# The first normalisation of x, taken from a second copy of x with channels on partitions

## The reference

```
x = x + tanh(g_xattn) * xattn(layernorm(x), ctx, ctx)        # 16 heads of 16, softmax, Wq Wk Wv Wo
x = x + tanh(g_ffn)   * ffn(layernorm(x))
layernorm(x) = (x - mean) / sqrt(var + 1e-5)                 # over the 256 channels, no weights
ffn(h):  h = bit_linear(h, w1)                               # 256 -> 1024
         h = depthwise_conv1d(h, 3 taps over positions) + b
         h = silu(h)
         return bit_linear(h, w2)                            # 1024 -> 256
bit_linear(x, w): x rounded to 8 bits per token, w to -1, 0, 1, then x @ w.T
```

## Time and profile before

| | |
|---|---|
| time of the runs | median 223.53 us, 222.73 to 223.77, 3 runs |
| profiled execution | 222.88 us, of which the span in the profile is 221.1 us |
| busy, share of the span | TensorE 92%, VectorE 82%, ScalarE 72%, GpSimd 62% |
| granted TensorE clock | 0.992 of full speed |
| largest chain shares | TensorE 64%, GpSimd 12%, VectorE 11% |
| DMA | 12.99 MB in 22159 packets, 59 GB/s over the span |

### The profile page before, as it was taken

One profiled execution on the slowest core, in us unless ns is written; L12 is line 12 of the kernel. 1 busy time (PEld: TensorE's weight loads), 2 busy tenths in 40 slices (PEclk: granted clock), 3 DMA queues, 4 the chain that ended last, 5 costly groups with the idle time before them and its releaser, 6 DMA issues.

```text
span 221.1 us, 6179 instructions
## 1 busy us (share of the span) xinstructions
PE 204.3 (92%) x2300; PEld 167.8 (76%) x2312; DVE 182.0 (82%) x375; ACT 160.1 (72%) x318; POOL 136.8 (62%) x241
## 2 busy tenths in 40 slices
PE   7999899999899999999999999999889849998894
PEld 7978778778688878788887878888558737786783
DVE  4154557698969899999999999999999989998982
ACT  2358677787678888897979888785689945875541
POOL 2502322553727575766758576675657998999971
PEclk9999999999999999999999999999999988999999
DMA  5992010101101010101100000000001222555543
GB/s 150 347 335 81 21 49 3 49 10 42 31 19 50 3 49 3 47 8 44 27 3 1 4 0 3 0 4 0 3 0 43 55 47 73 122 100 164 123 132 104
DMA packets 22159, 12.99 MB, mean 59 GB/s; under 512 B 13682, under 2 KB 21874, under 8 KB 22130
## 3 DMA queue, kind: packets, MB, share of 16 engines
q1 hardware_dynamic: 22130, 12.60, 20.0%
HBM read 7.36 MB, written 2.10 MB: 43 GB/s over the span
## 4 chain that ended last, share of the span: by engine, by line
PE 64%; POOL 12%; DVE 11%; issue 10%; ACT 1%; DMA 1%; POOLq 0%; ACTq 0%; DVEq 0%
PE ps_score L558 9%; PE ps_proj L524 8%; PE ps_proj L603 6%; PE ps_max L568 6%; PE ps_av L581 6%; PE ps_proj L516 5%; POOL y L415 5%; PE ps_proj L507 5%; PE ps_h L662 4%; POOL w2f L403 3%; PE ps_av L489 3%; DVE smax L1146 3%; PE ps_av L591 3%; PE ps_proj L495 2%; DVE zmax L1320 2%
## 5 line engine op out<-in xcount | busy, mean ns | idle before, releaser
L1146 DVE TENSOR_REDUCE smax<-ps_max 128x8 f32<-128x1024 f32 x31 | 37.9, 1224 | 14.1 <-PE ps_max L568 10.7
L910 ACT ACTIVATE prob<-ps_score 128x1024 f32<-128x1024 f32 x32 | 32.8, 1023 | 17.8 <-PE ps_score L558 16.9
L558 PE MATMUL ps_score<-Qs,KT 32*128 32x128 f32 x512 | 37.1, 283 | 2.0 <-DVE smax L1146 0.8
L558 PEld LDWEIGHTS ps_score<-Qs,KT 32*128 32x128 f32 x512 | 31.3, 186 | 9.3 <-issue 5.0
L568 PE MATMUL ps_max<-KT,QT 32*128 32x256 f32 x248 | 35.1, 400 | 0.0
L382 POOL TENSOR_SCALAR xn<-xn,qa 128x256 f32<-128x256 f32 x16 | 8.6, 535 | 27.0 <-DVE qa L1186 26.9
L568 PEld LDWEIGHTS ps_max<-KT,QT 32*128 32x128 f32 x248 | 21.2, 184 | 0.1
L403 POOL TENSOR_SCALAR w2f<-y,zmax 128x1024 f16<-128x1024 f32 x16 | 17.9, 1118 | 2.3 <-DVE zmax L1325 1.0
L1320 DVE TENSOR_REDUCE zmax<-y 128x1 f32<-128x1024 f32 x16 | 19.3, 1206 | 0.0
L524 PE MATMUL ps_proj<-xnT,wq 128*128 128x128 f32 x128 | 18.3, 286 | 0.9 <-ACT xnT L884 0.6
L1202 DVE SCALAR_TENSOR_TENSOR y<-hid,conv,y 128x508 f32<-128x508 f32 x24 | 19.1, 801 | 0.0
(11 more groups left out here) (147 smaller groups left out, 526.6 us busy)
## 6 DMA issues: line engine op xcount, KB each, us to landing
cin<-ctxT SPq DMA_DIRECT2D x16, 128.0 KB, 2.1
xres<-x SPq DMA_DIRECT2D x16, 128.0 KB, 2.5
out<-xres SPq DMA_DIRECT2D x16, 128.0 KB, 1.8
w1f<-w1T SPq DMA_DIRECT2D x1, 1024.0 KB, 7.0
w2f<-w2T SPq DMA_DIRECT2D x1, 1024.0 KB, 9.0
wk<-wkT SPq DMA_DIRECT2D x1, 256.0 KB, 2.8
wv<-wvT SPq DMA_DIRECT2D x1, 256.0 KB, 4.5
wq<-wqT SPq DMA_DIRECT2D x1, 256.0 KB, 4.7
```

The source lines that it names most:

```text
L558: mm = pe.matmul(ps_score[:, i * 512 + j * P:i * 512 + (j + 1) * P], KT[b % 3][rows, j * P:(j + 1) * P], Qs[rows, j * P:(j + 1) * P], star ...
L910: act.activation(prob[pair][:, :], ps_score[:, :], ACT.Exp, scale=DH ** -0.5).then_inc(exp_done, 1)
L1146: dve.tensor_reduce(dst, first_max(n, pair)[:, :].rearrange("p (g t e k) -> p g t e k", g=PG, t=KD, e=2), AX.X, ALU.max).then_inc(max_done, 1)
```

## The change

1. A second array `xT` comes in with each sequence of x laid out with channels on partitions. For sequences 4 to 15 (`BY_DMA = 4`) it is loaded into one of three buffers `xT` (`XB = 3`), and GpSimd normalises it there: one product with the factors, one sum with the shifts, both 128x256. project_q reads that buffer. TensorE's transposes and ScalarE's copy stay for sequences 0 to 3 only.
2. With channels on partitions, factor and shift differ along a row and are the same on all partitions. GpSimd makes them for several sequences at once (`norm_rows`, batches of 1, 1, 2, 4, 6 and 2 sequences, four small instructions each). For sequences 4 to 15 SP writes them to DRAM in three DMAs (`write_rows`), element by element, and loads two rows of 128 back for each sequence with all 128 partitions getting the same (`load_rows`), into one of two buffers `norm_bc`.
3. All statistics are VectorE's: those of sequences 2 to 13 in steps 0 to 2 and ahead of them, 14 and 15 in steps 7 and 8. ScalarE's sum_x and square_x are gone.
4. The last tap of tiles 1, 3, ... 17 is shared as those from 20 on: ScalarE makes the product behind its raw copy in the next step, and GpSimd adds it at the end of that step, behind norm1.
5. The loads of x come earlier, those of w2, of the small constants and of contexts 3 and on later; contexts 5 and on stand behind waits for `norm_ready` and `rows_out`.

```diff
+            def load_xT(n):
+                wait(sp, q_ready, n - XB + 1)
+                sp.dma_start(xT[n % XB][:, :], xTd[n * P:(n + 1) * P, :]).then_inc(xT_in[n % XB], 16)
+
+            def write_rows(first, last, ready):
+                sp.wait_ge(norm_ready, ready)
+                sp.dma_start(norm_dram[2 * first:2 * last, :].rearrange("r p -> p r"),
+                             norm_row[:, 2 * first:2 * last],
+                             allow_slow_non_contiguous=True).then_inc(rows_out, 16)
+
+            def load_rows(n, batches):
+                sp.wait_ge(rows_out, 16 * batches)
+                wait(sp, xn_done, n - 1 if n >= BY_DMA + 2 else 0)
+                sp.dma_start(norm_bc[n % 2][:, :],
+                             norm_dram[2 * n:2 * n + 2, :].rearrange("r p -> (r p)").partition_broadcast(P)
+                             ).then_inc(bc_in[n % 2], 16)
...
             load_x(2)
+            load_x(3)
             load_c(2)
+            load_x(4)
+            load_x(5)
+            load_c(3)
             load_w(w1f, w1T, KD, w1_in)
-            load_x(3)
-            load_c(3)
+            load_x(6)
+            load_x(7)
+            load_w(wo, woT, KD, wo_in)
+            for i in range(8, NB):
+                load_x(i)
+            sp.dma_start(conv[:, :], cwb).then_inc(small_in, 16)
             load_w(w2f, w2T, NC_, w2_in)
-            load_w(wo, woT, KD, wo_in)
-            sp.dma_start(conv[:, :], cwb).then_inc(small_in, 16)
-            for i in range(4, NB):
-                load_x(i)
-                load_c(i)
+            for n in range(BY_DMA, BY_DMA + XB):
+                load_xT(n)
+            load_c(4)
+            write_rows(4, 8, 4)
+            load_rows(4, 1)
+            load_rows(5, 1)
+            load_c(5)
+            load_c(6)
+            write_rows(8, 14, 5)
+            load_rows(6, 2)
+            load_c(7)
+            load_xT(7)
+            load_rows(7, 2)
+            for n in range(8, NB):
+                load_c(n)
+                load_xT(n)
+                if n == 14:
+                    write_rows(14, NB, 6)
+                load_rows(n, 2 if n < 14 else 3)
...
+            def norm_rows(first, last, batch):
+                k = slice(first, last)
...
+                gp.wait_ge(mv1_done, last)
+                gp.tensor_scalar(var1[:, k], var, EPS_LN, None, ALU.add).then_inc(norm_step, 1)
+                gp.wait_ge(norm_step, 3 * batch + 1)
+                gp.tensor_tensor(rstd, var1[:, k], minus_half[:, k], ALU.pow).then_inc(norm_step, 1)
+                gp.wait_ge(norm_step, 3 * batch + 2)
+                gp.tensor_tensor(mean_rstd1[:, k], mean, rstd, ALU.mult).then_inc(norm_step, 1)
+                gp.wait_ge(norm_step, 3 * batch + 3)
+                gp.tensor_scalar(shift, mean_rstd1[:, k], -1.0, 1.0, ALU.mult, ALU.mult).then_inc(norm_ready, 1)
...
             def norm1(i):
...
+                gp.wait_ge(xT_in[i % XB], 16 * ((i - BY_DMA) // XB + 1))
+                gp.wait_ge(bc_in[i % 2], 16 * ((i - BY_DMA) // 2 + 1))
+                gp.tensor_tensor(x3, x3, rstd, ALU.mult).then_inc(scaled_x, 1)
+                gp.wait_ge(scaled_x, i - BY_DMA + 1)
+                gp.tensor_tensor(x3, x3, shift, ALU.add).then_inc(xn_done, 1)
...
                 if seq(s + 2):
                     norm1(s + 2)
-                if seq(s + 3):
-                    gp.wait_ge(sh1_done, s + 3)
-                    x_mean(s + 3)
+                if s == 0:
+                    norm_rows(4, 8, 3)
+                if s == 2:
+                    norm_rows(8, 14, 4)
+                if s == 9:
+                    norm_rows(14, NB, 5)
+                for T in TILES.get(s - 1, ()):
+                    if tap_on_gp(T):
+                        add_tap(T)
...
             def project_q(n):
-                pe.wait_ge(xT_done, n + 1)
+                if n < BY_DMA:
+                    pe.wait_ge(xT_done, n + 1)
+                else:
+                    pe.wait_ge(xn_done, n + 1)
+                    pe.wait_ge(x1_done, n - 2)
...
                 for T in tiles[0:1]:
                     raw_copy(T)
+                for T in last[1:2]:
+                    if tap_on_gp(T):
+                        outer_product(T)
                 exponent(b, 0)
...
             def outer_taps(T):
                 first_tap(T)
-                last_tap(T)
+                if not tap_on_gp(T):
+                    last_tap(T)
...
+            stats_of(2, 3)
             row_max(0, 1)
-            step(0)
-            step(1)
+            step(0, lambda k: stats_of(4, 5) if k == 1 else None)
+            step(1, lambda k: stats_of(6, 7) if k == 0 else stats_of(8, 9))
...
+            def in_step2(k):
+                if k == 0:
+                    stats_of(10, 11)
+                else:
+                    weight_scale(0)
+                    stats_of(12, 13)
...
+            step(SB + 3, lambda k: stats_of(14) if k == 1 else None)
+            step(SB + 4, lambda k: stats_of(15) if k == 1 else None)
```

More of the change, by code:

```diff
@@ L49 @@
 ON_GP = 20
+BY_DMA = 4
+XB = 3
 BY_PE = 12
@@ L253, in turned, with tap_on_gp, tap_buffer @@
             return 16 * (v // ZT + 1)
+        def tap_on_gp(T):
+            return T >= ON_GP or T % 2 == 1 and T < ON_GP - 2
         def gp_taps(T):
-            return T - ON_GP + 1
+            return sum(tap_on_gp(t) for t in range(T + 1))
         def finished(eng, T):
-            eng.wait_ge(conv_done, min(T + 1, ON_GP))
+            eng.wait_ge(conv_done, T + 1 - gp_taps(T))
             wait(eng, conv_gp, gp_taps(T))
+        def tap_buffer(T):
+            return by_sequence(tap[gp_taps(T) % 2][:, :])[:, :, 0:P - 1]
         @block.sync
@@ new lines, in norm1 @@
+            def norm1(i):
+                if i < BY_DMA:
+                    gp.wait_ge(norm_ready, min(i, 2) + 1)
+                    wait(gp, xT_ready, i - 1)
+                    gp.tensor_scalar(xn[i % 2][:, :], xres[:, i * D:(i + 1) * D], norm_row[:, 2 * i:2 * i + 1],
+                                     norm_row[:, 2 * i + 1:2 * i + 2], ALU.mult, ALU.add).then_inc(xn_done, 1)
+                    return
+                x3 = xT[i % XB][:, :].rearrange("p (k n) -> p k n", n=P)
+                rstd, shift = (norm_bc[i % 2][:, e * P:(e + 1) * P].unsqueeze(1).broadcast_to([P, KD, P]) for e in range(2))
+                gp.wait_ge(xT_in[i % XB], 16 * ((i - BY_DMA) // XB + 1))
[3 more added lines that the diff above has]
+                gp.tensor_tensor(x3, x3, shift, ALU.add).then_inc(xn_done, 1)
@@ L520, in project_q @@
             def project_q(n):
-                pe.wait_ge(xT_done, n + 1)
+                if n < BY_DMA:
[3 more added lines that the diff above has]
+                    pe.wait_ge(x1_done, n - 2)
+                source = xnT if n < BY_DMA else xT[n % XB]
                 for t in range(KD):
@@ L524, in project_q @@
                         mm = pe.matmul(ps_q[:, t * P:(t + 1) * P], wq[:, k * D + t * P:k * D + (t + 1) * P],
-                                       xnT[:, k * P:(k + 1) * P], start=(k == 0), stop=(k == KD - 1))
+                                       source[:, k * P:(k + 1) * P], start=(k == 0), stop=(k == KD - 1))
                 mm.then_inc(q_ready, 1)
@@ L675, in step @@
                     weigh(a)
-                if seq(n):
+                if n < BY_DMA:
                     x_transpose(n)
@@ L952, in middle_tap, with outer_product @@
                                scale=conv[:, 4 * c + 1:4 * c + 2]).then_inc(tap1_done, 1)
+            def outer_product(T):
+                c = T % NC_
+                if T >= FOLDED:
+                    act.wait_ge(h_ready, T + 1)
+                    h3 = by_sequence(late_bank(T)[:, :])
+                else:
+                    act.wait_ge(scaled_dve, dve_tiles(T) + 1)
+                    h3 = by_sequence(hid[T % HB][:, :])
+                wait(act, conv_gp, gp_taps(T) - 2)
+                act.activation(tap_buffer(T), h3[:, :, 1:P], ACT.Copy,
+                               scale=conv[:, 4 * c + 2:4 * c + 3]).then_inc(tap2_done, 1)
             def w2_sums_copy():
@@ L999, in last_step @@
                 int_copy(d - 1)
+                outer_product(before[1])
                 exponent(b, 0)
@@ L1137, in norm_stats1, with stats_of @@
                 dve.wait_ge(st1_done, i + 1)
-                wait(dve, xn_done, i)
-                dve.bn_aggr(mv1[:, :], stats1[:, :]).then_inc(mv1_done, 1)
+                dve.bn_aggr(mv1[:, 2 * i:2 * i + 2], stats1[:, :]).then_inc(mv1_done, 1)
+            def stats_of(*sequences):
+                for i in sequences:
+                    norm_stats1(i)
             def row_max(n, pair):
```

104 lines of the change are left out of this document (33 added, 71 removed).

## The result

The changed kernel takes 234.28 us (median of 5 runs, 233.84 to 234.69) against 223.53 us (222.73 to 223.82): ratio 1.048, 95% interval 1.046 to 1.051. It is slower by 4.8%, outside my range of 217.7 to 223.3, on the side to which I gave a chance of 0.10. The profiled execution has a span of 232.8 us against 221.1.

What follows compares the result with a forecast made beforehand. TensorE, and close to it a loop through VectorE and GpSimd, were taken as bounds; -1.9 - 0.9 - 0.3 + 0.1 = -3.0 us took the span from 221.1 to 218.1, forecast 220.5 us, range 217.7 to 223.3.

Steps and rivals of the forecast that it cites:

- the queue of SP: SP's row writes, broadcasts and later context loads: writes take 3 to 5 us, hidden by 12 us of room.
- The rival of late rows: Row writes longer than 12 us stop GpSimd at norm1(4) and norm1(6), then TensorE at project_q: 232 us; chance 0.1.
- start: Normalising sequence 0 takes one more small GpSimd instruction: 0.1 us lost.
- steps 3 to 7: No add_tap meets a tap; transposes and copy wait go, partly offset by VectorE's statistics: 1.9 us gained of 2.35 possible.
- steps 8 to 14: Steady steps shorten from 9.63 to 9.50 us, 0.13 each, limited by the VectorE and GpSimd loop: 0.9 us gained.
- end: Last step: without tile 17's last_tap VectorE's queue runs up to 0.8 us earlier; 0.3 us gained, bounds 0 and 0.8.
- the first rival: Meeting of add_tap and tap costs nothing; steady steps of 9.16 gain 3.3 us in place of 0.9: 218.1 us; chance 0.2.
- The meeting: GpSimd's add_tap and VectorE's first outer tap, steps 8 to 14, exclude each other almost wholly; tap ends 0.53 us behind.
- the whole wait: Rival: VectorE's tap waits for all of add_tap, ending 0.73 us behind; steady steps 9.75, total 222.2 us; chance 0.05.
- My loop of 9.55: Steady-step loop through VectorE's taps and rounding and GpSimd's round1, norm1 and add_tap: six pieces sum to 9.55 us.
- ScalarE came at nothing: ScalarE's added tap product, 0.72 us before the first exponent, delays it 0.12 at most, covered: no cost.

Runs made afterwards that it cites:

- the runs with pieces: Each partition's elements written side by side: rows in the changed kernel (wrong values), 220.62 us; three added writes in the kernel before, 223.57 us.
- the kernel before with writes: Kernel before plus three writes of 12 x 128 single elements to DRAM, behind the loads of contexts 8, 11 and 14: 224.84 us, ratio 1.004.
- the run with both edits: Changed kernel with first three loads of turned x not waiting for project_q, and rows written in pieces (wrong values): 218.33 us, ratio 0.976.
- early loads: Changed kernel with only the needless wait of the first three loads of turned x taken away: 227.11 us, ratio 1.015.
- forms of write: Two kernels, each the kernel before plus transfers of different forms timed singly in SP's empty queue; totals not used; 1536 neighbouring single elements took 10.65 us.

## Why the prediction was wrong

**The step that failed** is the queue of SP, in two sentences of it. The first is "I take 3 to 5 us, hidden", for a write of rows. The writes took 10.9 and 11.9 us (the third 8.6), and they were not hidden. I had bounded them by a turned tile of as many packets, which is a transfer into SBUF. Nothing in the trace of before wrote single neighbouring elements to DRAM, so this row was no bound. The rival of late rows was right by half: GpSimd did stand idle behind the rows, for 10.69 us, but what TensorE waited for was context 4 in project_k, and no project_q waited. I had it decide "only beyond 12 us", because I looked only for who waits for the rows. At 10 to 12 us the write decides already, since something else is late while it is under way: context 4 in the first stop, TensorE's counts in the second. That is 6.4 + 6.6 us here. That both go with the form of the write is shown by the runs with pieces; how a write of single elements delays TensorE's counts, they don't show. The rival's figure of 232 was near by luck, since its two waits for rows are not the two stops.

The Trainium skill (DMA: Bandwidth & Descriptors, "Queues, rings and completion order") says that the increment by which a DMA engine reports a transfer lands only after every earlier write of that engine, across its queues. The runs agree for one queue (an x behind a write, 11.3 us in place of 2.1). Context 4 was issued half a microsecond ahead of the write and took 9.52 us. The rule need not be broken by that: the last 8 of its 256 packets moved at 36.0 to 36.7, and the write's single elements had begun at 34.4. In the kernel before with writes the contexts issued 0.38 us ahead of the three writes took 6.5, 2.3 and 2.1 us, so a transfer just ahead of a write is held in some cases only. The trace doesn't tell packets by DMA engine, so the runs can't decide it.

The second failed sentence is that the rows of sequences 4 to 7 "are written from about 23.4". GpSimd did have them at 24, but load_xT(6) waits for q_ready of 4, at 33.0, ahead of load_c(4) and write_rows(4, 8). I had asked what stands behind the writes, and not what stands in front of them. It took away the 10 us of room and cost 3.25 us by itself.

**Held against the run with both edits** (span 216.6, from 221.1), the other terms can be read:

| term | predicted | measured |
|---|---|---|
| start | +0.1 | +0.05 |
| steps 3 to 7 | -1.9 | -1.8 |
| steps 8 to 14 | -0.9 | -3.3 |
| end | -0.3 | +0.6 |
| sum | -3.0 | -4.5 |

At 218.3 us this kernel lies in my range but 2.2 under the forecast, next to the first rival's 218.1. The sum of the changed kernel then closes: -4.5 for this, +9.6 and +6.6 for the two stops, against +11.7 of span.

**Steps 8 to 14** went as the first rival had it, though by another road. The meeting costs what the earlier trace rows said. Timelines of VectorE (the first outer tap and Q's shifts), GpSimd (the first of its two instructions of 128x256, and add_tap) and TensorE (project_out, row stage), all in step 8 of the changed kernel:

```profile
103.79 1.11 DVE L1260 SCALAR_TENSOR_TENSOR y<-hid,conv,y 128x508 f32<-128x508 f32 x1
...
105.61 0.87 DVE L1211 SCALAR_TENSOR_TENSOR Qs<-ps_score,max_row,QT 128x256 f32<-128x256 f32 x2
...
101.57 0.73 POOL L418 TENSOR_TENSOR xT<-xT,norm_bc 128x256 f32<-128x256 f32 x1
...
103.06 1.30 POOL L471 TENSOR_TENSOR y<-y,tap 128x508 f32<-128x508 f32 x1
...
101.21 1.13 PE L672 MATMUL ps_proj<-wo,attT 128*128 128x256 f32 x4
...
106.53 0.38 PE L627 MATMUL ps_score<-Qs,KT 32*128 32x128 f32 x2
```

Add_tap ends at 104.36 and the tap that it met at 104.90, 0.54 behind, and in all seven of the steps 8 to 14 it is 0.54 or 0.55 (predicted 0.53; the whole wait, and with it the rule of the Trainium skill (SBUF — State Buffer, "Who interferes with whom") taken literally, would have been 0.73; the measurement decides). A 128x256 instruction of GpSimd took 0.73 (predicted 0.72). What was off is small. GpSimd starts them at t = 0.36 in place of 0.48, and the two take 1.49 with their gaps in place of 1.62. So add_tap ends at t = 3.15, the tap at 3.69 and the shifts of Q at 5.27, 0.05 before TensorE wants them, where I had 5.49 and 5.34. My loop of 9.55 is one of 9.14 by the trace. Its six pieces, in my order, last 2.15, 2.73, 0.94, 1.48, 1.29 and 0.54 us where I had 2.26, 2.80, 1.06, 1.62, 1.28 and 0.53. So four of them were put 0.07 to 0.14 too long. Only the 0.07 can have been a wait for TensorE, in front of the row maximum; the rest lies in the gaps between instructions, which are other ones in the new order. By that the loop is as long as TensorE's own work, 9.16, and these runs don't tell which of the two sets the step.

**The end** had the wrong sign. The share of tile 17 doesn't spare VectorE a tap there, but puts GpSimd's add beside VectorE's last tap of tile 18: 1.63 us in place of 0.84, and TensorE waits 1.33 in place of 0.73. Timelines of TensorE, VectorE and GpSimd:

```profile
176.60 0.60 PE L731 MATMUL ps_h<-xqT,w1q 128*128 128x512 bf16 x2 [1.33 <-DVE hid L1251]
...
174.31 1.63 DVE L1267 SCALAR_TENSOR_TENSOR y<-hid,conv,y 128x508 f32<-128x508 f32 x1
...
173.62 1.77 POOL L471 TENSOR_TENSOR y<-y,tap 128x508 f32<-128x508 f32 x1
```

I had met two such meetings in the earlier trace rows and looked for a third only in the steady steps. The run that keeps tile 17 on VectorE, and the share alone in the kernel before, show it from both sides.

ScalarE came at nothing, as predicted: its product takes 0.71, and its exponent follows without a wait (step 10).

## What to carry to other kernels

A transfer of small elements is not priced by its packets alone: direction, size and neighbours in DRAM decide, and 128 words of 4 bytes cost as much as 7.3 us or as little as 1.4. Before hiding a slow transfer, ask what else is late while it is under way (here a load, and the counts of an engine that has nothing to do with it), and not only who waits for its data; and read an in-order queue in front of an instruction as carefully as behind it. A wait that guards the reuse of a buffer should not be there on its first use.

## What the runs showed of the hardware

- Writes from SBUF to DRAM of single elements of 4 bytes, neighbours from different partitions: 7.3, 8.0 and 10.65 us for 128, 512 and 1536 in an empty queue. Set 64 bytes apart, 1.4 us for 128 and 4.7 for 1536. Of the 10.65 us, the packets of single elements take 147.72 to 148.69, within 2 us of the issue at 146.80; in the changed kernel's second write they take 53.57 to 54.55 of 52.66 to 64.53, and no packet but two of instructions moves behind them.
- While such a write is under way, a load of 128 KB issued just behind it took 9.5 and 11.3 us in place of 2 to 3. Of those issued 0.4 to 0.5 us ahead of one, one took 9.5, one 6.5 and two 2.1 to 2.3.
- Under five such writes (one in the changed kernel, two with early loads, one in the kernel before with writes, one with forms of write) TensorE's semaphore counts came up to 1.7, 2.4, 3.0, 3.3 and 5.7 us behind the ends of its matmuls as the profile models them, and the engines that needed them stood still. Under the others, and in all runs without one, none came more than 0.15 us behind.
- A tap on VectorE that meets an add on GpSimd ends 0.54 to 0.55 us behind it; behind a product of GpSimd in the kernel before it was 0.53.
